# Order of TensorE's work at the end of the attention, in a cross-attention and two-layer local-attention block

## The chip, the cores and the metric

The kernel runs on one core of one Trainium2 chip. The metric is the device time of one execution in microseconds (us); the median of several runs is compared.

## The reference, cut to what matters

There are eight sequences of 256 rows by 256 columns, all float32. A gated cross-attention comes first. Then a small transformer of two layers runs over every sequence. One layer, cut to its core (H is 8 heads of 64, the window is 128 rows, and the hidden width of the feed-forward part is 682):

```python
h = shift_token(x)
q, k, v = split(h @ wqkv)
q, k = rotary_xpos(l2norm(q) * qs, l2norm(k) * ksc)
o = local_attention(q, k, v)
x = x + o @ wo                                   # "output product"
h = layernorm(shift_token(x)) * lg + lb
a, g = split(h @ w1 + b1)
x = x + (a * gelu(g)) @ w2 + b2                  # "down product"
```

## The kernel before, in words

Every engine has an instruction stream written out by hand, and semaphores hold the streams together; there is no scheduler. After the cross-attention come 17 **steps** (`run_steps`, each engine has its own `step(s, la, lf)`). Step s does two things at once: the attention of item s (`la` is its layer) and the feed-forward part of item s-1 (`lf` is its layer). Items 0 to 7 are the eight sequences in layer 0, items 8 to 15 are the same in layer 1. Step 0 has attention only (`lf` is None), steps 1 to 8 have `lf` 0, steps 9 to 15 have `lf` 1, and step 16 has the feed-forward part only. Steps 2 to 7 and 9 to 14 are hardware loops; the others are written out.

The weight products run as three float32r matmuls for each product (`split_product`, line 422): high by high, high by low, low by high. So each activation and each weight exists as a high part (`_hi`, copied by ScalarE) and a low part (`_lo`, subtracted by VectorE or GpSimd).

The end of a step on TensorE, in the order of the code: for each head h, `tr_probs(h)` (lines 609 to 611) transposes the probabilities; after every second head `weighted(pair)` (lines 623, 627) multiplies them by the values; pieces of the down product of item s-1 (`down(n)`, 12 pieces of three matmuls) stand between them. Behind the last head, 7, come `weighted(3)`, the four transposes of the next item's rows (`y_next`, line 415, PSUM bank 0), the last two down pieces (10 and 11, bank 7), and then the output product: two row tiles by four pairs of heads by three matmuls, 24 matmuls, row tile outermost, all in bank 2.

The three other engines at this place, each in this order:

- ScalarE: `heads_out(3)` (line 871) copies the result of `weighted(3)` as `oT_hi`; then `evac_yT` (line 800) copies the transposed next rows as `yT_hi`; in steps 0 and 8 `high_parts` (line 754) then copies the high parts of the next feed-forward weights.
- VectorE: `low_oT(3)` (line 1150) makes `oT_lo`; `low_yT` (line 1054) makes `yT_lo`; line 1259 adds the residual to the down product (called **yo** below); where `lf` is 1, line 1263 applies the gate and the second residual (**yo2**); line 1270 adds the residual to the output product and gives **x1**; in steps 0 and 8 `low_parts` (line 1039) then makes the low parts of the first feed-forward layer's weights.
- SyncE issues the loads and stores: the store of the finished rows waits for `res_done`, the load of `y_res` for `x1_done`, and the load of `y_next` for `y_tr`.

The next step begins on TensorE with `project(0, (0,))` (six matmuls of 512 columns, waits for `yT_done`), then `shift_rows` (lines 645 to 647, waits for x1), then the other projections. VectorE waits for `shift_rows` and starts its row statistics (line 1175); from these GpSimd and ScalarE make the normalised rows `hn` (line 883), which TensorE transposes.

Of the kernel before, what the change touches and what calls it, by code (L numbers as in the profile page):

```python
# [18 lines left out]
P = 128  # L19
# [3 lines left out]
ALU = mybir.AluOpType  # L23
# [6 lines left out]
HEADS, DH = 8, 64  # L30
# [4 lines left out]
def wait(eng, semaphore, value):  # L35

    if isinstance(value, int) and value <= 0:
        return
    eng.wait_ge(semaphore, value)
# [10 lines left out]
def build(nc, x, ctx_in, mask, g_xattn, g_ffn, Wq, bq, Wk, bk, Wv, bv, ln_gamma, ln_beta,  # L50
          wqkv, q_scale, k_scale, wo, ln_g, ln_b, w1, b1, w2, b2, rot_tab, win_mask, ident_in, shift_in, out):
    NB, S, D = x.shape
    T = S // P
# [3 lines left out]
    PAIRS = HEADS // 2  # L57
# [7 lines left out]
    STEPS = DEPTH * NB  # L65
# [10 lines left out]
    with st:  # L76
        def sb(name, shape, dt=F32):
            return st.enter_context(nc.sbuf_tensor(name, shape, dt))

        def sem(name):  # L80
            return st.enter_context(nc.semaphore(name))
# [5 lines left out]
        wo_hl = [sb(f"wo_{n}", [P, PAIRS, D], F32R) for n in ("hi", "lo")]  # L87
# [43 lines left out]
        y_next = sb("y_next", [P, T, D])  # L131
        y_res = sb("y_res", [P, T, D])
# [15 lines left out]
        oT = [sb(f"oT_{n}", [P, PAIRS, S], F32R) for n in ("hi", "lo")]  # L148
        x1 = sb("x1", [P, T, D])
# [13 lines left out]
        ps = st.enter_context(nc.psum_tensor("ps", [P, 8, 512], F32))  # L163

        def bank(i):
            return ps[:, i, :]

        def halves(i):
            return ps[:, i, :].rearrange("p (t n) -> p t n", t=2)
# [23 lines left out]
        ynext_in, yres_in, xm_in, res_stored = (  # L193
            sem(n) for n in ("ynext_in", "yres_in", "xm_in", "res_stored"))
# [213 lines left out]
        def _(pe):  # L408
            mm = nc.tensor.matmul

            def transpose_rows(src, b):

                for k in range(KC):
                    for t in range(T):
                        last = nc.tensor.transpose(bank(b)[:, k * S + t * P:k * S + t * P + P],  # L415
                                                   src[:, t, k * P:(k + 1) * P], ident[:])
                return last

            def split_product(out, lhsT, rhs, start, stop):

                for i, (a, b) in enumerate(((0, 0), (0, 1), (1, 0))):
                    last = mm(out, lhsT(a), rhs(b), start=(start and i == 0), stop=(stop and i == 2))  # L422
                return last
# [98 lines left out]
            def step(s, la, lf):  # L522
                f = s - 1

                def project(t, parts):

                    i = 0 if t == 0 else 3
                    if t == 0 and 0 in parts:
                        pe.wait_ge(yT_done, s + 1)
                        if isinstance(s, int) and s == 0:  # L530
                            pe.wait_ge(xnT_done, NB)
                            pe.wait_ge(kT_x, KC * NB)
                            pe.wait_ge(qT_x, KC * NB)
                            pe.wait_ge(v_x, NB)
                    elif 0 in parts:
                        wait(pe, pT_done, HEADS * s)
                    for j in parts:
                        if j == 2:
                            if t == 0:
                                wait(pe, x1_done, s)  # L540
                            else:
                                wait(pe, o_done, PAIRS * s)
                        if t == 0 and isinstance(s, int) and s in (0, NB):
                            pe.wait_ge(w_ready, VPIECES * la + j + 1)
                        o = bank(i + j) if j < 2 else bank(2 + 4 * t)
                        for k in range(KC):
                            c0 = k * YTC - k + t * P
                            last = split_product(o, lambda a: yT[a][:, c0:c0 + P],
                                                 lambda a: wqkv_hl[a][:, k, j * INNER:(j + 1) * INNER],
                                                 k == 0, k == KC - 1)  # L550
                        last.then_inc((qk_mm, qk_mm, v_mm2)[j], 1)
# [35 lines left out]
                def scores_own(pair):  # L587

                    for h in (2 * pair, 2 * pair + 1):
                        if h >= SB:  # L590
                            pe.wait_ge(mn_done, T * (HEADS * s + h - SB + 1))
                    for h in (2 * pair, 2 * pair + 1):
                        r = slice(h % 2 * DH, h % 2 * DH + DH)
                        mm(bank(h % SB)[:, 0:P], qT[r, pair, 0:P], kT[r, pair, 0:P], start=True, stop=True)  # L594

                def scores_both(pair):

                    for h in (2 * pair, 2 * pair + 1):
                        r = slice(h % 2 * DH, h % 2 * DH + DH)
                        mm(bank(h % SB)[:, P:3 * P], qT[r, pair, P:S], kT[r, pair, :], start=True, stop=True)\  # L600
                            .then_inc(s_mm2, 1)

                def tr_probs(h):

                    b, p = bank(3 + h % 2), pr[:, h % NS, :]
                    pe.wait_ge(pn_done, T * (HEADS * s + h + 1))
                    if h >= 2:
                        pe.wait_ge(pT_done, HEADS * s + h - 1)
                    nc.tensor.transpose(b[:, 0:P], p[:, 2 * P:3 * P], ident[:])  # L609
                    nc.tensor.transpose(b[:, P:2 * P], p[:, 0:P], ident[:])  # L610
                    nc.tensor.transpose(b[:, 2 * P:3 * P], p[:, P:2 * P], ident[:]).then_inc(pt_tr, 1)  # L611
# [41 lines left out]
                if A:  # L653
                    project(0, (0,))
                if F:
                    shift_rows()
                if A:
                    project(0, (1,))
# [31 lines left out]
                def downs(upto):  # L690

                    nonlocal n
                    while F and n < upto:
                        down(n)
                        n += 1

                if A:
                    pe.wait_ge(q_done, s + 1)
                    pe.wait_ge(k_done, T * s + 1)
                    pe.wait_ge(v_done, T * (s + 1))  # L700
                    scores_own(0)
                    pe.wait_ge(q1_done, s + 1)
                    pe.wait_ge(k_done, T * (s + 1))
                    scores_both(0)
                    downs(5)
                    for h in range(HEADS + 1):
                        if h in (0, 1, 3):
                            scores_own((h + 3) // 2)
                            scores_both((h + 3) // 2)
                        if h == 0:  # L710
                            downs(7)
                        if h < HEADS:
                            tr_probs(h)
                        if isinstance(s, int) and s in (0, NB) and h == HEADS - 1:
                            bias_products(la)
                        downs(min(10, 7 + (h + 1) // 2))
                        if h and h % 2 == 0:
                            weighted(h // 2 - 1)
                    if not (isinstance(s, int) and s == STEPS - 1):
                        pe.wait_ge(ynext_in, 16 * (s + 2))  # L720
                        pe.wait_ge(mn_done, T * HEADS * (s + 1))
                        transpose_rows(y_next, 0).then_inc(y_tr, 1)
                if F:
                    while n < T * HC:
                        down(n)
                        n += 1
                if A:
                    pe.wait_ge(o_done, PAIRS * (s + 1))
                    if isinstance(s, int) and s in (0, NB):
                        pe.wait_ge(w_ready, VPIECES * la + FIRST)  # L730
                        pe.wait_ge(b1_done, 3 * (la + 1))
                    for t in range(T):
                        for c in range(PAIRS):
                            last = split_product(bank(2)[:, t * D:(t + 1) * D],
                                                 lambda a: oT[a][:, c, t * P:(t + 1) * P],
                                                 lambda a: wo_hl[a][:, c, :], c == 0, c == PAIRS - 1)
                    last.then_inc(wo_mm, 1)

            run_steps(pe, step)


# [202 lines left out]
        def _(dve):  # L944
            V = nc.vector
# [130 lines left out]
            def step(s, la, lf):  # L1076
# [188 lines left out]
                if A:  # L1265
                    dve.wait_ge(wo_mm, s + 1)
                    dve.wait_ge(yres_in, 16 * (s + 1))
                    wait(dve, hn_done, s)
                    wait(dve, xb_done, s)
                    V.tensor_tensor(x1[:], halves(2), y_res[:], ALU.add).then_inc(x1_done, 1)  # L1270
                if isinstance(s, int) and s in (0, NB):
                    dve.wait_ge(b1_done, 3 * (la + 1))
                    low_parts(la, False, slice(LAST_W2 - FIRST, None))
# [192 lines left out]
```

## Time and profile before

| | us |
|---|---|
| median of 3 runs | 802.25 |
| lowest and highest run | 800.89, 802.79 |
| the profiled execution, its own time | 802.92 |
| its span, first to last instruction | 801.1 |

The mean granted TensorE clock of the profiled execution is 0.964 of full speed. The page gives busy times of each engine over the span; a timeline gives single instructions in order of time: start, duration, engine, line, operation, what is written and read, how many are merged in the row, and in brackets the idle time of the engine before it with what ended it. PE is TensorE's matmuls, PEld its weight loads, DVE is VectorE, ACT is ScalarE, POOL is GpSimd. Starts of neighbouring rows give the pace of an engine better than durations do, since instructions of one engine overlap at their ends.

### The profile page before, as it was taken

What the parts mean: (1) busy time and instruction counts of PE and PEld (TensorE: products, weight loads), DVE (VectorE), ACT (ScalarE), POOL (GpSimd) and SP (SyncE); (2) the same over time, 40 slices, a digit from 0 to 9 for tenths busy, and PEclk for the clock granted to TensorE, in tenths of its full rate; (3) what the DMA queues carried; (4) which work ended last, traced back from release to release, by engine and by line L of the source; (5) the groups of instructions that cost most, each with busy time, mean ns of one, the idle gap of its engine ahead of it and who ended that gap; (6) DMA issues with size and microseconds to landing.
All of it is one profiled execution on the core that took longest, in us unless ns stands there. A gap on an engine that the chain in (4) does not pass through costs nothing.

```text
span 801.1 us, 17081 instructions
## 1 busy us (share of the span) xinstructions
PE 726.8 (91%) x4984; PEld 604.8 (75%) x4984; DVE 532.6 (66%) x1486; ACT 481.9 (60%) x1289; POOL 439.9 (55%) x592
## 2 busy tenths in 40 slices
PE   6998875999999999999999899999999999999967
PEld 5787753777878787878787779778787878787846
DVE  2888897285858585757585854858585857575732
ACT  2333523468585858585757683757575757575842
POOL 0433553375556565656574564838383847474722
PEclk9999985799999999999999997999999999999999
DMA  6444330460101010101010101010101010101000
GB/s 213 145 144 157 111 65 27 133 226 13 41 2 39 0 39 0 39 0 39 0 39 1 39 2 53 1 54 0 52 0 52 0 52 0 52 0 40 1 27 13
DMA packets 32786, 38.36 MB, mean 48 GB/s; under 512 B 8476, under 2 KB 22896, under 8 KB 32752
## 3 DMA queue, kind: packets, MB, share of 16 engines
q1 hardware_dynamic: 32752, 37.95, 14.9%
q8 instruction: 16, 0.26, 0.1%
q14 instruction: 18, 0.15, 0.1%
HBM read 29.55 MB, written 8.39 MB: 47 GB/s over the span
## 4 chain that ended last, share of the span: by engine, by line
PE 55%; ACT 9%; issue 7%; DVE 7%; POOL 3%; DMA 1%; DVEq 0%; SPq 0%; ACTq 0%; POOLq 0%
PE ps L422 35%; PE ps L623 4%; ACT pr L860 4%; PE ps L582 3%; PE ps L609 2%; PE ps L600 2%; PE ps L517 2%; PE ps L594 2%; POOL pr L1372 2%; ACT pT L866 1%; PE ps L415 1%; DVE hT_lo L1130 1%; PE ps L627 1%; ACT hT_hi L899 1%; DVE sm L1157 1%
## 5 line engine op out<-in xcount | busy, mean ns | idle before, releaser
L1372 POOL TENSOR_SCALAR pr<-pr,rl 128x128 f32<-128x128 f32 (+1 forms) x256 | 106.9, 432 | 56.8 <-DVE rl L1163 56.5
L860 ACT ACTIVATE pr<-sm,mn 128x128 f32<-128x128 f32 (+1 forms) x256 | 113.8, 448 | 15.6 <-DVE mn L1157 14.5
L422 PE MATMUL ps<-hT_hi,w_hi 128*128 128x256 f32 (+1 forms) x352 | 105.0, 298 | 3.5 <-DVE hT_lo L1130 1.4
L1157 DVE CUSTOM_DVE_ANT_0 sm<-ps,wmask 128x128 f32<-128x128 f32 (+1 forms) x256 | 80.1, 355 | 34.5 <-PE ps L600 30.5
L422 PE MATMUL ps<-hT_hi,w_lo 128*128 128x256 f32 (+1 forms) x352 | 99.8, 284 | 0.0
L422 PE MATMUL ps<-hT_lo,w_hi 128*128 128x256 f32 (+1 forms) x352 | 99.0, 281 | 0.0
L1340 POOL TENSOR_TENSOR rn<-ss,nhalf 128x16 f32<-128x16 f32 x32 | 95.2, 2974 | 2.7
L820 ACT ACTIVATE sqb<-ps 128x512 f32<-128x512 f32 x64 | 38.0, 596 | 94.3 <-PE ps L422 88.6
L1354 POOL TENSOR_TENSOR u_lo<-u_pair,u_hi 128x256 fp32r<-128x256 f32 x64 | 74.1, 1166 | 25.3 <-ACT u_hi L841 15.6
L422 PE MATMUL ps<-wqkv_hi,yT_hi 128*128 128x512 f32 x192 | 80.0, 417 | 7.8 <-DVE arena L1002 5.3
L1285 POOL TENSOR_SCALAR hrs<-hmv 128x2 f32<-128x2 f32 x16 | 3.1, 193 | 151.5 <-DVE hmv L1180 151.5
L422 PE MATMUL ps<-wqkv_hi,yT_lo 128*128 128x512 f32 x192 | 77.2, 402 | 0.0
L422 PE MATMUL ps<-wqkv_lo,yT_hi 128*128 128x512 f32 x192 | 77.1, 402 | 0.0
L422 PEld LDWEIGHTS ps<-hT_hi,w_hi 128*128 128x128 f32 (+1 forms) x352 | 66.3, 188 | 11.0 <-DVE hT_lo L1130 10.4
L832 ACT ACTIVATE gl<-ps,b_sb 128x256 f32<-128x256 f32 x80 | 38.1, 476 | 53.6 <-PE ps L422 53.6
L422 PEld LDWEIGHTS ps<-hT_lo,w_hi 128*128 128x128 f32 (+1 forms) x352 | 66.8, 190 | 0.0
L422 PEld LDWEIGHTS ps<-hT_hi,w_lo 128*128 128x128 f32 (+1 forms) x352 | 66.2, 188 | 0.0
L422 PE MATMUL ps<-w_hi,u_hi 128*128 128x256 f32 x192 | 62.8, 327 | 0.7 <-POOL u_lo L1354 0.7
L866 ACT ACTIVATE pT<-ps 128x384 f32<-128x384 f32 x128 | 61.5, 483 | 2.4 <-PE ps L611 0.9
L1150 DVE TENSOR_TENSOR oT_lo<-ps,oT_hi 128x256 fp32r<-128x256 f32 x64 | 27.1, 424 | 48.8 <-ACT oT_hi L871 47.2
L422 PE MATMUL ps<-w_hi,u_lo 128*128 128x256 f32 x192 | 54.2, 282 | 0.0
L623 PE MATMUL ps<-pT,vs 128*64 128x256 f32 x256 | 42.7, 412 | 12.4 <-ACT pT L866 9.0
(150 smaller groups left out, 2098.0 us busy)
## 6 DMA issues: line engine op xcount, KB each, us to landing
arena<-x SPq DMA_DIRECT2D x16, 256.0 KB, 3.4
ystream<-arena SPq DMA_DIRECT2D x16, 256.0 KB, 2.1
y_next<-ystream SPq DMA_DIRECT2D x16, 256.0 KB, 2.7
y_res<-ystream SPq DMA_DIRECT2D x16, 256.0 KB, 2.6
arena<-L_ffn_w SPq DMA_DIRECT2D x6, 640.0 KB
arena<-ctx SPq DMA_DIRECT2D x8, 256.0 KB, 3.8
arena<-mask_BxSxS_ik SPq DMA_DIRECT2D x8, 256.0 KB, 2.8
xmid<-arena SPq DMA_DIRECT2D x8, 256.0 KB, 2.0
```

The costliest lines, as they stand in the source:

```text
L422: last = mm(out, lhsT(a), rhs(b), start=(start and i == 0), stop=(stop and i == 2))
L582: last = nc.tensor.transpose(bank(i + j)[:, c * P:(c + 1) * P], t1[:, t, j * INNER + c * P:j * INNER + (c + 1) * P], ident[:])
L623: mm(b[j * DH:(j + 1) * DH, 0:S], vs[:, 0, h * DH:(h + 1) * DH], pT[:, h % 4, P:3 * P], start=True, stop=False)
L820: A(sqb[:, j * INNER:(j + 1) * INNER], bank(i + j), ACT.Square).then_inc(sq_done, 1)
L832: A(gl[:, c % 2, :], ps[:, 5 + c % 2, S:2 * S], ACT.Gelu, bias=b1_sb[:, lf, 1, c:c + 1]).then_inc(gl_done, 1)
L860: A(pr[:, h % NS, a:b], sm[:, h % NS, a:b], ACT.Exp, bias=mn[:, h, t:t + 1], scale=-1.0, accum_out=ls[:, h, t:t + 1]).then_inc(e_done, 1)
L866: A(pT[:, h % 4, :], bank(3 + h % 2)[:, 0:3 * P], ACT.Copy).then_inc(pT_done, 1)
L1150: V.tensor_tensor(oT[1][:, pair, :], bank(5 + pair % 2)[:, 0:S], oT[0][:, pair, :].bitcast(F32), ALU.subtract).then_inc(o_done, 1)
L1157: V.tensor_tensor_reduce(sm[:, h % NS, a:b], bank(h % SB)[:, a:b], wmask[:, a:b], 1.0, -NEG, ALU.add, ALU.min, mn[:, h, t:t + 1]).then_inc ...
L1340: G.tensor_tensor(rn[:, t, :], ss[:, t, :], nhalf[:], ALU.pow).then_inc(rn_done, 1)
L1354: G.tensor_tensor(u[1][0:r, c, :], u_full[c % 4][0:r, :], u[0][0:r, c, :].bitcast(F32), ALU.subtract).then_inc(u_done, 1)
L1372: G.tensor_scalar(pr[:, h % NS, a:b], pr[:, h % NS, a:b], rl[:, h, t:t + 1], 1.0, ALU.mult, ALU.mult).then_inc(pn_done, 1)
```

## The change

`weighted(3)` leaves the loop over the heads. Behind the last transposes of probabilities now stand: the last two down pieces, the transposes of the next rows, the output product of pairs 0 and 1, `weighted(3)`, and the output product of pairs 2 and 3. The output product takes the pair as its outer loop and the row tile as its inner one, with row tile 0 in bank 1 and row tile 1 in bank 2; before each pair it waits for that pair's `o_done` alone. x1 (line 1270 before) reads the two banks. `project` gets a wait for `x1_done` ahead of the second projection of the first row tile, which uses bank 1. Nothing is added or removed: the same matmuls run in another order. The other engines' streams stay as they are, but for the operand of x1.

```diff
                     for j in parts:
+                        if j == 1 and t == 0:
+                            wait(pe, x1_done, s)
                         if j == 2:
...
-                        if h and h % 2 == 0:
+                        if h and h % 2 == 0 and h < HEADS:
                             weighted(h // 2 - 1)
+                if F:
+                    while n < T * HC:
+                        down(n)
+                        n += 1
+                if A:
                     if not (isinstance(s, int) and s == STEPS - 1):
                         pe.wait_ge(ynext_in, 16 * (s + 2))
                         pe.wait_ge(mn_done, T * HEADS * (s + 1))
                         transpose_rows(y_next, 0).then_inc(y_tr, 1)
-                if F:
-                    while n < T * HC:
-                        down(n)
-                        n += 1
-                if A:
-                    pe.wait_ge(o_done, PAIRS * (s + 1))
+
+                    def out_products(pairs):
+
+                        for c in pairs:
+                            pe.wait_ge(o_done, PAIRS * s + c + 1)
+                            for t in range(T):
+                                last = split_product(bank(1 + t)[:, 0:D],
+                                                     lambda a: oT[a][:, c, t * P:(t + 1) * P],
+                                                     lambda a: wo_hl[a][:, c, :], c == 0, c == PAIRS - 1)
+                        return last
+
+                    pe.wait_ge(mn_done, T * HEADS * (s + 1))
                     if isinstance(s, int) and s in (0, NB):
                         pe.wait_ge(w_ready, VPIECES * la + FIRST)
                         pe.wait_ge(b1_done, 3 * (la + 1))
-                    for t in range(T):
-                        for c in range(PAIRS):
-                            last = split_product(bank(2)[:, t * D:(t + 1) * D],
-                                                 lambda a: oT[a][:, c, t * P:(t + 1) * P],
-                                                 lambda a: wo_hl[a][:, c, :], c == 0, c == PAIRS - 1)
-                    last.then_inc(wo_mm, 1)
+                    out_products(range(0, 2))
+                    weighted(PAIRS - 1)
+                    out_products(range(2, PAIRS)).then_inc(wo_mm, 1)
...
-                    V.tensor_tensor(x1[:], halves(2), y_res[:], ALU.add).then_inc(x1_done, 1)
+                    V.tensor_tensor(x1[:], ps[:, 1:1 + T, 0:D], y_res[:], ALU.add).then_inc(x1_done, 1)
```

TensorE's stream before, at the end of a layer-1 loop step (steps 9 to 14), from the transposes of head 7 on; `w2` rows are down pieces, `wo` rows the output product:

```order
L609 MATMUL ps<-ident,pr 128x128
L610 MATMUL ps<-ident,pr 128x128
L611 MATMUL ps<-ident,pr 128x128
L618 REGISTER_ALU
L623 MATMUL ps<-pT,vs 64x256 x2
L627 MATMUL ps<-pT,vs 64x128 x2
L720 ISA
L721 REGISTER_ALU
L415 MATMUL ps<-ident,y_next 128x128 x4
L422 MATMUL ps<-w2_hi,u_hi 128x256
```

Behind the last row stand the rest of the two down pieces and the 24 output matmuls. The same stream with the change, first the transposes of the next rows and what follows them, in which the output product of pair 0 begins:

```order
L422 MATMUL ps<-w2_hi,u_lo 128x256
L727 ISA
L728 REGISTER_ALU
L415 MATMUL ps<-ident,y_next 128x128 x4
L422 MATMUL ps<-wo_hi,oT_hi 128x256
L422 MATMUL ps<-wo_lo,oT_hi 128x256
L422 MATMUL ps<-wo_hi,oT_lo 128x256
```

The down pieces and the transposes now stand ahead of `weighted(3)`. Then the place where `weighted(3)` stands now, between pair 1 and pair 2 of the output product:

```order
L422 MATMUL ps<-wo_hi,oT_lo 128x256
L625 MATMUL ps<-pT,vs 64x256 x2
L629 MATMUL ps<-pT,vs 64x128 x2
L734 REGISTER_ALU
L422 MATMUL ps<-wo_hi,oT_hi 128x256
```

Twelve output matmuls stand ahead of `weighted(3)`, twelve behind it. VectorE's stream at the same place, as it stands before (with the change the order is the same and only the line numbers are higher by 10), for a step with `lf` 1:

```order
L1150 TENSOR_TENSOR oT_lo<-ps,oT_hi 128x256
L1052 REGISTER_ALU
L1054 TENSOR_TENSOR yT_lo<-ps,yT_hi 128x2x256
L39 REGISTER_ALU
L1259 TENSOR_TENSOR arena<-ps,arena 128x512
L1261 REGISTER_ALU
L1262 REGISTER_ALU
L1263 SCALAR_TENSOR_TENSOR arena<-arena,tg 128x512
L1267 REGISTER_ALU
L1270 TENSOR_TENSOR x1<-ps,y_res 128x512
```

Nothing moved here: yT_lo, yo, yo2 and x1 stand behind oT_lo of pair 3, as before.

## Rows read from the trace of the kernel before

**Rows 1.** The page, busy time of each engine, and the chain that ended last by engine.

```profile
PE 726.8 (91%) x4984; PEld 604.8 (75%) x4984; DVE 532.6 (66%) x1486; ACT 481.9 (60%) x1289; POOL 439.9 (55%) x592
...
PE 55%; ACT 9%; issue 7%; DVE 7%; POOL 3%; DMA 1%; DVEq 0%; SPq 0%; ACTq 0%; POOLq 0%
```

**Rows 2.** Timeline of PE, end of step 12 and start of step 13.

```profile
645.87 0.27 PE L611 MATMUL ps<-ident,pr 128*128 128x128 f32 x1
645.90 0.36 PE L422 MATMUL ps<-w_hi,u_hi 128*128 128x256 f32 x1
...
648.23 0.27 PE L611 MATMUL ps<-ident,pr 128*128 128x128 f32 x1
649.16 0.65 PE L623 MATMUL ps<-pT,vs 128*64 128x256 f32 x4 [0.66 <-ACT pT L866]
...
649.96 0.66 PE L415 MATMUL ps<-ident,y_next 128*128 128x128 f32 x4
650.37 0.36 PE L422 MATMUL ps<-w_hi,u_hi 128*128 128x256 f32 x1
...
651.15 0.28 PE L422 MATMUL ps<-wo_hi,oT_hi 128*128 128x256 f32 x1
...
654.00 0.39 PE L422 MATMUL ps<-wqkv_hi,yT_hi 128*128 128x512 f32 x1
...
655.39 0.38 PE L645 MATMUL ps<-x,shift 128*128 128x128 f32 x2
```

**Rows 3.** Timeline of ACT, the same step.

```profile
646.27 0.37 ACT L871 ACTIVATE oT_hi<-ps 128x256 fp32r<-128x256 f32 x1
646.54 0.94 ACT L866 ACTIVATE pT<-ps 128x384 f32<-128x384 f32 x2
...
650.09 0.38 ACT L871 ACTIVATE oT_hi<-ps 128x256 fp32r<-128x256 f32 x1 [1.07 <-PE ps L627]
650.65 0.60 ACT L800 ACTIVATE yT_hi<-ps 128x512 fp32r<-128x512 f32 x1 [0.17 <-PE ps L415]
```

**Rows 4.** Timeline of DVE: x1 of step 11, then the same step 12 (`lf` 1).

```profile
614.82 0.69 DVE L1270 TENSOR_TENSOR x<-ps,y_res 128x512 f32<-128x512 f32 x1 [0.94 <-PE ps L422]
...
650.51 0.42 DVE L1150 TENSOR_TENSOR oT_lo<-ps,oT_hi 128x256 fp32r<-128x256 f32 x1 [1.58 <-ACT oT_hi L871]
651.28 0.69 DVE L1054 TENSOR_TENSOR yT_lo<-ps,yT_hi 128x512 fp32r<-128x512 f32 x1 [0.35 <-ACT yT_hi L800]
651.89 0.68 DVE L1259 TENSOR_TENSOR arena<-ps,arena 128x512 f32<-128x512 f32 x1
652.70 0.75 DVE L1263 SCALAR_TENSOR_TENSOR arena<-arena,tg 128x512 f32<-128x512 f32 x1
654.39 0.69 DVE L1270 TENSOR_TENSOR x<-ps,y_res 128x512 f32<-128x512 f32 x1 [0.94 <-PE ps L422]
```

**Rows 5.** Timeline of DVE, x1 at the end of step 2 (`lf` 0).

```profile
243.53 0.69 DVE L1270 TENSOR_TENSOR x<-ps,y_res 128x512 f32<-128x512 f32 x1 [1.82 <-PE ps L422]
```

**Rows 6.** Timeline of PE, end of step 15 (no transposes of next rows).

```profile
767.83 0.65 PE L623 MATMUL ps<-pT,vs 128*64 128x256 f32 x4 [0.58 <-ACT pT L866]
...
769.67 0.39 PE L422 MATMUL ps<-wo_hi,oT_hi 128*128 128x256 f32 x1
...
773.56 0.49 PE L645 MATMUL ps<-x,shift 128*128 128x128 f32 x2 [0.78 <-DVE x L1270]
```

**Rows 7.** End of step 8 and start of step 9: PE, ACT, DVE, PE.

```profile
486.19 1.12 PE L623 MATMUL ps<-pT,vs 128*64 128x256 f32 x4
...
490.17 4.10 ACT L754 ACTIVATE w_hi<-arena 128x1280 fp32r<-128x1280 f32 x4 [0.74 <-PE ps L422]
...
494.23 3.78 DVE L1039 TENSOR_TENSOR w_lo<-arena,w_hi 128x1386 fp32r<-128x1386 f32 x2
...
502.93 0.66 PE L415 MATMUL ps<-ident,hn 128*128 128x128 f32 x4 [1.70 <-ACT hn L883]
```

**Rows 8.** Busy times by stretch, step 8: us and busy us per engine, then PEclk, DMA share, GB/s.

```profile
486.00:489.00 3.00, 3.00 (x16) 2.27 (x16) 0.81 (x4) 0.56 (x2) 2.53 (x2) 0.50 0.00 0
```

More of the change, by code:

```diff
@@ L716, in step @@
                         downs(min(10, 7 + (h + 1) // 2))
-                        if h and h % 2 == 0:
+                        if h and h % 2 == 0 and h < HEADS:
                             weighted(h // 2 - 1)
[L719 to L722, printed above, removed]
                 if F:
@@ L727, in step @@
                 if A:
-                    pe.wait_ge(o_done, PAIRS * (s + 1))
+                    if not (isinstance(s, int) and s == STEPS - 1):
+                        pe.wait_ge(ynext_in, 16 * (s + 2))
+                        pe.wait_ge(mn_done, T * HEADS * (s + 1))
+                        transpose_rows(y_next, 0).then_inc(y_tr, 1)
+                    def out_products(pairs):
[6 more added lines that the diff above has]
+                        return last
+                    pe.wait_ge(mn_done, T * HEADS * (s + 1))
                     if isinstance(s, int) and s in (0, NB):
```

## The prediction, as made before the change was measured

> **What bounds the kernel now.** I read the page first [rows 1]: TensorE is busy for 91% of the span and holds 55% of the chain that ended last, twice as much as ScalarE, VectorE, GpSimd and the issue time together. So the time is the length of TensorE's stream, and a change is worth what it takes out of TensorE's idle time less what it puts in. From the x1 of step 11 to that of step 12, 614.82 to 654.39, are 39.57 us [rows 4], and the other loop steps repeat it, so one step can stand for many, and small sums count by the number of steps.
>
> Then I read the end of one loop step on each engine. On TensorE [rows 2] the last transpose of probabilities starts at 648.23, and `weighted(3)` only at 649.16, with 0.66 us idle in front of it: it waits for ScalarE's copy pT. That is the hole that the change can fill. Behind it TensorE has no gap: next rows, two down pieces, 24 output matmuls, the next step's first projection at 654.00, and `shift_rows` at 655.39. On VectorE [rows 4] oT_lo, yT_lo, yo and yo2 follow `weighted(3)` one after another, and x1 comes after 0.94 us of idle time. With `lf` 0 there is no yo2 and the idle time is 1.82 us [rows 5]. These two numbers are VectorE's slack against TensorE, and the change spends it, since all of that work stands behind `weighted(3)`, which comes later now.
>
> **The sum for one loop step.** W is the start of `weighted(3)`; before, it is 649.16.
>
> 1. TensorE up to W. Down pieces may start 0.03 us behind the start of the last transpose, as 645.87 to 645.90 shows. Two of them take 650.37 to 651.15, 0.78. The four transposes take 649.96 to 650.37, 0.41. Twelve output matmuls take half of 651.15 to 654.00, 1.42, and 0.08 more since the first product behind transposes is slower (0.78 against 0.71 for six) [rows 2]. A switch to the small products of `weighted` I price at 0.09 by the same kind of penalty, between 0 and 0.2. So W is 648.23 + 0.03 + 0.78 + 0.41 + 1.50 + 0.09 = 651.04, 1.88 later than before. pT is ready long before: the idle time of 0.66 us is gone.
> 2. TensorE behind W. Only pair 2's six matmuls are ready there. Pair 3 needs ScalarE and VectorE first. The end of step 15 shows exactly this pattern, `weighted(3)`, six matmuls, then a wait for oT_lo: from 767.83 to 769.67, 1.84 us [rows 6]. Six more take 0.78, so the next step's first projection could start at W + 2.62 = 653.66 against 654.00. Of the 0.66 us hole and the pause around it, about a third of a microsecond is left as gain; the rest comes back as a new wait for pair 3 and two more switches between kinds of products.
> 3. The same moment by yT. `heads_out(3)` starts 0.93 behind W (650.09 less 649.16). Its wait for the transposes of the next rows is gone, so yT_hi starts 0.27 later, the distance between 646.27 and 646.54, takes 0.60, and yT_lo starts 0.03 after it, as now (650.65 + 0.60 to 651.28), so at W + 1.83 [rows 3, 4]. It ends at W + 2.52, just in time for W + 2.62. There is 0.1 us to spare.
> 4. x1 with `lf` 0. yo comes 0.61 after yT_lo, at W + 2.44, and x1 another 0.61 later, at W + 3.05; it ends at W + 3.74. `shift_rows` follows six projections, 1.39 us (654.00 to 655.39), so at W + 4.01 = 655.05. x1 is ready. **Gain 0.34 us per step**; I take 0.32, between 0.1 and 0.4.
> 5. x1 with `lf` 1. yo2 comes 0.81 behind yo, at W + 3.25. x1 needs the engine, 0.67 later (0.75 less the overlap of 0.08 that 651.28, 0.69 long, and 651.89 show): W + 3.92. It ends at W + 4.61, and `shift_rows` starts 0.05 later, at 655.70 (as in step 15, where it follows a late x1) [rows 4, 6], with a first product slower by some 0.1, an estimate by the penalty of item 1. In effect `shift_rows` is finished as if it had begun at 655.81, against 655.39. **Loss 0.42 us per step.** TensorE stands idle for about 0.6 us in front of `shift_rows` instead of in front of `weighted(3)`. Everything of the next step hangs on `shift_rows` or on TensorE's order behind it, so the loss isn't made up. Bounds: 0.1 if everything on VectorE runs closer than the rows show, 0.7 if nothing overlaps.
>
> A rule of the Trainium skill bears on item 5: "VectorE: DVE Perf Modes", section "The DRAIN you can't avoid", says that the next operation on VectorE does not start until the pipe of the one before is empty. By that rule alone the step would lose about 0.2 us more. The trace does not follow it to the letter here, with starts 0.61 us apart for operations of 0.69 us (yT_lo and yo) [rows 4].
>
> **The steps that are not in that pattern.** In step 15 there are no next rows, and x1 waits for nothing but yo2 and the products; by the same items it gains 0.3. Behind steps 0 and 8 the high parts of the weights stand on ScalarE behind yT_hi, and VectorE's low parts need the third of them before the row statistics can begin. TensorE waits for what follows, 1.70 us in step 9 [rows 7], so a delay there counts in full. In step 8 the clock is at 0.50 of full, which is the 1.2 GHz level [rows 8], because the bias products of single columns came before; the run ahead of W, 2.69 us at full clock, takes about 4.9 there (estimate, 1.8 times). W is then 486.19 + 4.9 = 491.1, the high parts start 0.93 + 0.27 + 0.5 later, at 492.8 instead of 490.17, and the third ends about 2.75 us on, at 495.5. The low parts began at 494.23 [rows 7]. **Loss 1.3 in step 8.** In step 0 no down pieces stand ahead: I take 0.8. Both lie between 0 and 2; a clock that rises sooner, since dense products come sooner, makes them smaller.
>
> The added wait for x1 in `project` costs nothing: `shift_rows`, ahead of it, waits for the same. The two banks cost nothing either: one instruction reads both, and it waits for the last product anyway. SyncE's store of the finished rows moves back with yo2 by over 1 us, and the load of `y_res` behind it has most of a step before it is needed; `y_next` is asked for behind x1 too.
>
> **Sum.** Seven steps with `lf` 0 (1 to 7): -2.2. Step 15: -0.3. Six steps with `lf` 1 (9 to 14): +2.5. Step 0: +0.8. Step 8: +1.3. Together +2.1 us. On the profiled execution's 802.92 that is 805.0, on the median of the runs, 0.7 below it, 804.4. About 0.2%, 1.6 us, is what a measurement of this kernel can tell from no change.
>
> **Rivals.**
>
> - A, faster: VectorE and ScalarE keep up in all steps, and each of 15 steps keeps 0.32 us. Against it speak the 0.94 us of slack with `lf` 1, of which W moving back by 1.88 asks twice as much; for it, that TensorE is the engine of the chain. 802.25 - 4.8 = 797.5. The Trainium skill's "Perfetto Trace Analysis", section "Optimization Strategies", argues this way: the goal is a matmul engine as highly utilized as possible. It would have the filled hole count as a gain. Chance 0.15.
> - B, no change: steps 1 to 15 as summed, but behind steps 0 and 8 the clock rises sooner or the delayed weights find cover. -2.2 - 0.3 + 2.5 = 0, so 802.3. Chance 0.15.
> - C, clearly slower: also with `lf` 0 x1 or yT_lo comes too late. There yT_lo has 0.1 us to spare and x1 0.2, so if VectorE's chain is longer by over 0.2 us from W, the gain of seven steps goes and `lf` 1 loses 0.6. 6 x 0.6 and the 2.1 of steps 0 and 8 are +5.7: 808. Chance 0.12. The Trainium skill's rule quoted in item 5 leads here, if it held in full.
> - D, the hole isn't filled, because another wait holds TensorE ahead of W. Of the output product's operands oT_lo of pair 1 would be the one; it is done over 1 us before its use. Under 0.03.
>
> My forecast, slower through late x1 and late weights while `lf` 0 steps gain, has 0.55. Its own range is 802.5 to 806.5, a third of it within 0.2%.
>
> **Chances and range.** Faster: A and a little of the forecast's edge, 0.17. Same: B and a third of the forecast, 0.30. Slower: the rest with C, 0.53. The predicted time is the forecast's 804.4. The range from 800.2 to 807.0 takes in B and most of C and leaves out A.
>
> **What the changed profile should show.** No idle time in front of `weighted(3)`, which starts 1.9 us later behind the last transpose; about 0.2 us idle in front of pair 3's first product; with `lf` 1 about 0.6 us idle in front of `shift_rows`, released by x1, and no idle time in front of x1 but full occupation from yT_lo on; with `lf` 0 no wait at `shift_rows`. Loop steps of 39.25 us with `lf` 0 and 40.0 with `lf` 1, against 39.57. A longer wait for hn in steps 1 and 9. I am wrong if the layer-1 steps are shorter than before, or if step 9 doesn't start its statistics later.

## The result, and the profile after the change

| | before | changed |
|---|---|---|
| median, us | 802.52 (6 runs) | 809.44 (6 runs) |
| lowest and highest run | 800.89, 805.09 | 806.8, 812.93 |
| the profiled execution, its own time | 802.92 | 812.93 |
| its span | 801.1 | 811.0 |
| its mean granted clock | 0.964 | 0.955 |

Changed over before is 1.0099, with a 95% interval of 1.0078 to 1.0119: slower by 6.9 us. The prediction said 804.4, and its range ended at 807.0. The profiled execution of the changed kernel is the slowest of its six, 3.5 us over their median. So its parts below add up to more than 6.9.

The page of the changed kernel, busy times and chain by engine:

```profile
PE 736.0 (91%) x4984; PEld 611.3 (75%) x4984; DVE 533.8 (66%) x1486; ACT 479.4 (59%) x1289; POOL 436.7 (54%) x592
...
PE 53%; ACT 10%; DVE 8%; issue 8%; POOL 3%; DMA 1%; DVEq 1%; ACTq 0%; SPq 0%; POOLq 0%
```

Against [rows 1] the same 4984 matmuls are busy for 9.2 us longer. Part of that is the order itself. These are the windows from one x1 to the next of a layer-1 loop step, first of the kernel before, then of the changed one (columns as in [rows 8]; the clock is at 1.00 in both):

```profile
614.82:654.39 39.57, 38.03 (x282) 31.61 (x281) 27.23 (x78) 26.90 (x74) 23.91 (x32) 1.00 0.09 27
622.66:662.71 40.05, 38.61 (x282) 31.72 (x280) 27.14 (x79) 26.75 (x74) 23.85 (x32) 1.00 0.08 26
```

TensorE is busy 0.58 us longer per step with `lf` 1, and with `lf` 0 it is 38.36 against 38.01. Over steps 1 to 7 and 9 to 14 that makes about 6 of the 9.2 us (estimate). So busy time tells little here; the mean clock, 0.955 against 0.964, is the better hint.

**A loop step.** TensorE at the end of step 12, timeline, answering to [rows 2]:

```profile
655.98 0.27 PE L613 MATMUL ps<-ident,pr 128*128 128x128 f32 x1
656.01 0.37 PE L422 MATMUL ps<-w_hi,u_hi 128*128 128x256 f32 x1
...
658.77 0.65 PE L625 MATMUL ps<-pT,vs 128*64 128x256 f32 x4
...
659.57 0.38 PE L422 MATMUL ps<-wo_hi,oT_hi 128*128 128x256 f32 x1
...
660.26 0.28 PE L422 MATMUL ps<-wo_hi,oT_lo 128*128 128x256 f32 x1
660.61 0.38 PE L422 MATMUL ps<-wo_hi,oT_hi 128*128 128x256 f32 x1
...
661.42 0.45 PE L422 MATMUL ps<-wqkv_hi,yT_hi 128*128 128x512 f32 x1
...
663.52 0.48 PE L647 MATMUL ps<-x,shift 128*128 128x128 f32 x2 [0.49 <-DVE x L1280]
```

The hole in front of `weighted(3)` is gone, and a new one of 0.49 us stands at `shift_rows`, released by x1. VectorE in the same step, answering to [rows 4]:

```profile
660.13 0.42 DVE L1160 TENSOR_TENSOR oT_lo<-ps,oT_hi 128x256 fp32r<-128x256 f32 x1 [3.44 <-ACT oT_hi L881]
660.62 0.69 DVE L1064 TENSOR_TENSOR yT_lo<-ps,yT_hi 128x512 fp32r<-128x512 f32 x1
661.23 0.68 DVE L1269 TENSOR_TENSOR arena<-ps,arena 128x512 f32<-128x512 f32 x1
662.04 0.75 DVE L1273 SCALAR_TENSOR_TENSOR arena<-arena,tg 128x512 f32<-128x512 f32 x1
662.71 0.68 DVE L1280 TENSOR_TENSOR x<-ps,y_res 128x512 f32<-128x512 f32 x1
```

From yT_lo to x1 the profile shows no wait. Between one x1 and the next lie 39.27 us with `lf` 0 and 40.04 with `lf` 1, against 39.57 before. Six steps of +0.47, seven of -0.30 and the -0.56 of step 15 come to +0.2, close to the forecast 0. So the 6.9 us are not here.

**Steps 0 and 8.** The distances from x1 to x1 show the place. Step 1 takes 44.38 us (before 41.58), and step 9 takes 46.87 (before 42.06). Timeline of VectorE at the end of step 8, with the row statistics of step 9 behind it, answering to [rows 7]:

```profile
495.70 0.68 DVE L1280 TENSOR_TENSOR x<-ps,y_res 128x512 f32<-128x512 f32 x1
497.27 4.91 DVE L1049 TENSOR_TENSOR w_lo<-arena,w_hi 128x1386 fp32r<-128x1386 f32 x2 [0.89 <-ACT w_hi L764]
502.11 0.28 DVE L1185 BATCH_NORM_STATS2 hst<-x 128x6 f32<-128x128 f32 x1
```

ScalarE, GpSimd and TensorE at the same place:

```profile
494.34 4.08 ACT L764 ACTIVATE w_hi<-arena 128x1280 fp32r<-128x1280 f32 x4
495.70 5.02 POOL L1377 TENSOR_TENSOR w_lo<-arena,w_hi 128x1280 fp32r<-128x1280 f32 x2 [4.81 <-ACT w_hi L764]
...
507.10 1.12 PE L415 MATMUL ps<-ident,hn 128*128 128x128 f32 x4 [3.95 <-ACT hn L893]
```

The low parts of the weights are late, as forecast. But they also take 4.91 us where they took 3.78, and TensorE's wait for hn is 3.95 us where it was 1.70 [rows 7]. The windows of the changed kernel (columns as in [rows 8]):

```profile
495.00:500.00 5.00, 5.00 (x28) 4.25 (x28) 4.11 (x4) 4.50 (x6) 4.30 (x2) 1.00 0.54 193
500.00:505.00 5.00, 3.15 (x14) 2.22 (x12) 4.96 (x11) 0.60 (x1) 1.82 (x4) 1.00 0.06 18
505.00:510.00 5.00, 2.90 (x9) 2.52 (x10) 4.35 (x7) 4.27 (x8) 4.65 (x4) 0.62 0.00 0
510.00:515.00 5.00, 5.00 (x31) 4.81 (x31) 3.63 (x6) 1.70 (x5) 3.99 (x2) 0.70 0.01 3
```

And of the kernel before, over the same stage:

```profile
500.00:505.00 5.00, 3.29 (x16) 2.10 (x14) 4.67 (x8) 4.15 (x9) 4.59 (x6) 1.00 0.00 0
505.00:510.00 5.00, 4.89 (x40) 4.78 (x41) 4.94 (x9) 3.08 (x7) 4.75 (x3) 1.00 0.01 3
510.00:515.00 5.00, 5.00 (x44) 4.85 (x42) 4.22 (x7) 3.50 (x9) 4.76 (x5) 1.00 0.00 2
```

The granted clock is at the 1.2 GHz level for part of the last two stretches. Before, with the short wait, it stayed at full. The counts of matmuls, 40 against 84, are not of the same work, since this stage begins 4.2 us later in the changed kernel. The clock falls while TensorE still waits, about 1 us before the transposes of hn:

```profile
506.00:507.00 1.00, 0.00 (x0) 0.00 (x0) 0.96 (x3) 1.00 (x4) 1.00 (x1) 0.60 0.00 0
```

### The profile page after: what moved, and what is told of

It is laid out like the page before. It is cut to its first block, busy times and chain, and to the rows that moved or that the text cites. A ratio compares the mean times of both kernels' runs of the same rounds, so it can differ in the third digit from the quotient of the medians.

```text
span 811.0 us, 17122 instructions
## 1 busy us (share of the span) xinstructions
PE 736.0 (91%) x4984; PEld 611.3 (75%) x4984; DVE 533.8 (66%) x1486; ACT 479.4 (59%) x1289; POOL 436.7 (54%) x592
## 2 busy tenths in 40 slices
DMA packets 32786, 38.36 MB, mean 47 GB/s; under 512 B 8476, under 2 KB 22896, under 8 KB 32752
## 4 chain that ended last, share of the span: by engine, by line
PE 53%; ACT 10%; DVE 8%; issue 8%; POOL 3%; DMA 1%; DVEq 1%; ACTq 0%; SPq 0%; POOLq 0%
PE ps L422 33%; ACT pr L870 4%; PE ps L625 3%; PE ps L584 3%; PE ps L611 2%; PE ps L602 2%; PE ps L517 2%; PE ps L596 2%; POOL pr L1382 2%; PE ps L629 1%; PE ps L415 1%; DVE hT_lo L1140 1%; DVE sm L1167 1%; ACT hT_hi L909 1%; DVE oT_lo L1160 1%
## 5 line engine op out<-in xcount | busy, mean ns | idle before, releaser
L422 PEld LDWEIGHTS ps<-hT_hi,w_hi 128*128 128x128 f32 (+1 forms) x352 | 68.0, 193 | 9.5 <-DVE hT_lo L1140 9.3
L881 ACT ACTIVATE oT_hi<-ps 128x256 fp32r<-128x256 f32 x64 | 24.0, 376 | 74.7 <-PE ps L629 74.7
```

## The experiments

Two theories stood at the start. **W:** the loss comes from steps 0 and 8, through the late weights. **L:** it comes from the loop steps, through the late x1 of layer 1.

### 1. The new order everywhere but in steps 0 and 8

```diff
-                    out_products(range(0, 2))
-                    weighted(PAIRS - 1)
-                    out_products(range(2, PAIRS)).then_inc(wo_mm, 1)
+                    if (isinstance(s, int) and s in (0, NB)):
+                        pe.wait_ge(o_done, PAIRS * (s + 1))
+                        out_products(range(PAIRS)).then_inc(wo_mm, 1)
+                    else:
...
```

The last down pieces and `weighted(3)` have their old places in these two steps too.

> The change in all steps but 0 and 8, which keep the order of before (products still in two banks). Theory W (nearly all of the loss comes from the late weight parts behind steps 0 and 8 and what follows in steps 1 and 9): 802.5 us, between 801 and 804, with steps 1 and 9 as long as before (41.6 and 42.1 us from x1 to x1), since steps 1 to 7 and 15 gain 2.5 us and steps 9 to 14 lose 2.5 to 2.9. Rival L (the late x1 in the layer-1 loop costs most): over 806 us.

Measured: 802.08 against 802.23, ratio 1.0002 (0.9987 to 1.0017). The loop steps are as in the changed kernel (39.27 and 40.04), and steps 1 and 9 take 41.01 and 42.65 us. **Theory W holds, and L falls.** Thirteen new loop steps and step 15 cost nothing in sum that the measurement could tell.

### 2. The new order in steps 0 and 8 alone

The condition of the first experiment turned round.

> The new order only in steps 0 and 8, the order of before in all others. Theory W: 808 to 810 us, steps 1 and 9 together 6 to 8 us longer than before, with a wait for the normalised rows of over 3.5 us in both. Rival L: at most 803 us.

Measured: 808.35, ratio 1.0089 (1.0066 to 1.0112), 6.1 us more than before. Steps 1 and 9 take 45.63 and 45.05 us, together 7.0 more than before, and TensorE waits 3.70 and 3.95 us for hn in them. Two steps of seventeen make nearly the whole loss.

### 3. High parts of the weights first

```diff
+                    if isinstance(s, int) and s in (0, NB):
+                        high_parts(la, False)
                     heads_out(PAIRS - 1)
                     ...
-                if isinstance(s, int) and s in (0, NB):
-                    high_parts(la, False)
```

The change, but ScalarE makes the high parts ahead of the copies of `weighted(3)`, in the time in which it has nothing to do.

> The change, and in steps 0 and 8 ScalarE copies the high parts of the feed-forward weights before it copies the result of the last weighted values, while it would sit idle. Theory W: the loss of steps 1 and 9 goes, 801 to 803 us; VectorE's two low parts, which no longer overlap with GpSimd's, take under 3.5 us where they took 4.91, and the wait for the normalised rows is under 2 us. Rival L: 808 us, no gain of over 1.5.

Measured: 800.26, ratio 0.9983 (0.9962 to 1.0004); against the changed kernel's 809.44 that is 9.2 us. The interval takes in 1, so this kernel can't be called faster than the one before. Step 1 takes 40.98 us and step 9 takes 41.93. The low parts now take 3.10 us for the same two operations. The tile `w_lo` in step 0, in the changed kernel (durations in ns, minimum, median and maximum, then first and last start):

```profile
L1377 POOL TENSOR_TENSOR w_lo<-arena,w_hi x2: 2118/2538/2959, 163.2 to 166.1; 128x1280 fp32r<-128x1280 f32 x1, 42x256 fp32r<-42x256 f32 x1
L1049 DVE TENSOR_TENSOR w_lo<-arena,w_hi x2: 2142/2495/2848, 164.7 to 167.5; 128x1386 fp32r<-128x1386 f32 x2
```

And in this experiment, where GpSimd's part is over before VectorE's begins:

```profile
L1377 POOL TENSOR_TENSOR w_lo<-arena,w_hi x2: 726/1824/2921, 158.4 to 161.2; 128x1280 fp32r<-128x1280 f32 x1, 42x256 fp32r<-42x256 f32 x1
L1049 DVE TENSOR_TENSOR w_lo<-arena,w_hi x2: 1592/1594/1597, 163.0 to 164.5; 128x1386 fp32r<-128x1386 f32 x2
```

Alone, VectorE needs 1.60 us for one and GpSimd 2.92 and 0.73. Together they seem to take turns. GpSimd's first runs from 163.16 to 166.12. VectorE's first, started at 164.73, ends at 164.73 + 2.85 = 167.58, 1.46 behind that. GpSimd's small one starts at 166.1 and ends at 168.2, 0.65 behind VectorE's first. VectorE's second ends at 169.64, 1.4 behind that. Each end is the end of the other engine's operation plus nearly the full length of one's own. This can be tested by itself (experiment 9).

### 4. x1 ahead of yo2

```diff
-                    if lf == 1:
-                        ... yo2 ...
                     V.tensor_tensor(x1[:], ps[:, 1:1 + T, 0:D], y_res[:], ALU.add).then_inc(x1_done, 1)
+                if lf == 1:
+                    ... yo2 ...
```

> The change, and VectorE makes x1 before the second residual of the finished rows (yo2) where lf is 1. By the rows, each of steps 9 to 14 loses its late x1 (0.45 us) and keeps the gain of the layer-0 steps (0.3 us): 6 x 0.75 = 4.5 us less than the change, 804 to 806 us; loop steps of 39.27 us in layer 1. Rival: if something else than x1 holds shift_rows in layer 1, no more than 1 us less than the change.

Measured: 809.01, ratio 1.0086 (1.006 to 1.0112). The expectation failed. Layer-1 steps fell only from 40.04 to 39.74, and TensorE's timeline in step 12 says why:

```profile
660.24 0.49 PE L647 MATMUL ps<-x,shift 128*128 128x128 f32 x2 [0.19 <-DVE arena L1279]
```

The releaser is now yo2, not x1: `shift_rows` also waits for `res_done`, which in layer 1 only yo2 sets. I had moved one of two operations that TensorE waits for. The 6 x 0.30 us that the trace shows as gain are not to be seen in the time, 809.01 against 809.44; the intervals of the two ratios are wider than the difference.

### 5. Both mends, with the wait put right

```diff
                     pe.wait_ge(x1_done, s)
-                    wait(pe, res_done, f)
+                    if lf == 1:
+                        pe.wait_ge(yo_done, s - NB)
+                    else:
+                        wait(pe, res_done, f)
```

Experiments 3 and 4 together. `res_done` guards bank 7 here, which yo has read already, so `yo_done` is enough (its count gets one added in step 8, where yo still counts for `res_done`).

> Both mends: ScalarE's high parts first in steps 0 and 8, x1 ahead of yo2, and shift_rows waits in layer 1 for yo instead of yo2 (bank 7 is free from yo on; in the kernel with x1 first it was yo2 that released shift_rows, 0.19 us late, and the loop steps took 39.74 us). Theory: layer-1 loop steps take 39.27 us as those of layer 0, 0.77 less than with the change; 6 x 0.77 = 4.6 us below the kernel with the high parts first (800.3): 795 to 797 us. Rival: a third wait takes the place (yT_lo), and the steps stay over 39.6: 798 to 800 us.

Measured: **796.24**, ratio 0.9925 (0.991 to 0.994), faster than both kernels. Steps 1 and 9 take 40.99 and 41.16 us, and the layer-1 steps 39.39. Against the third experiment layer 1 gives 6 x 0.64 = 3.8 us by the trace, and 4.0 by the times (800.26 less 796.24). The time came out as expected, though the steps did not quite reach the expected 39.27. The new order of VectorE's end of a step:

```profile
646.60 0.68 DVE L1272 TENSOR_TENSOR arena<-ps,arena 128x512 f32<-128x512 f32 x1
647.19 0.68 DVE L1278 TENSOR_TENSOR x<-ps,y_res 128x512 f32<-128x512 f32 x1
647.79 0.74 DVE L1282 SCALAR_TENSOR_TENSOR arena<-arena,tg 128x512 f32<-128x512 f32 x1
```

`shift_rows` then starts at 648.24 without a wait for yo2.

### 6. The kernel before, with late weights

```diff
                 if isinstance(s, int) and s in (0, NB):
+                    act.wait_ge(wo_mm, s + 1)
                     high_parts(la, False)
```

TensorE's order is the old one, and the high parts wait for the output product.

> The kernel before, in which ScalarE in steps 0 and 8 waits for the end of the output product before it copies the high parts, about 3.5 us later than it did. No instruction on TensorE moves. If late weight parts alone make the loss of steps 1 and 9, both get longer by 2.5 to 5 us and the whole is 807 to 811 us; if it takes the new order on TensorE too, it stays under 804 us.

Measured: 811.97, ratio 1.0124 (1.0105 to 1.0142), 9.6 us slower, a little over what was expected. Late weights make the loss without any new order. The low parts take 4.90 us here too, and steps 1 and 9 take 46.43 and 47.19.

### 7 and 8. What the clock adds

The seventh is the changed kernel with step 9 written out in front of the loop, nothing else. It is the control for the eighth, which has this in steps 1 and 9, ahead of the transposes of hn:

```diff
+                if isinstance(s, int) and s in (1, NB + 1):
+                    for i in range(12):
+                        mm(bank(5), yT[0][:, 0:P], wqkv_hl[0][:, 0, 0:INNER], start=True, stop=True)
```

These twelve products are added work that nobody reads; they fill most of the wait.

> Control for the next: the change with step 9 written out instead of being the loop's first turn. 807 to 811 us, as the change; steps 1 and 9 long as there, clock at half after the wait for the normalised rows.

> The same with 12 products of 512 columns into the unused bank 5 in steps 1 and 9, ahead of the transposes of the normalised rows, where TensorE sits idle for 3.7 to 3.95 us; they take 2.8 us and their result is used nowhere. If part of the loss is the clock that falls in that wait, it stays at full speed, and steps 1 and 9 get shorter by 1 to 2.5 us together or each: 2 to 4 us less than the control. If the clock plays no part: the same time.

Measured: 807.99, ratio 1.0073 (1.0051 to 1.0095), and with the fill 807.0, ratio 1.0057 (1.0033 to 1.0082). The times don't tell the two apart. The traces do, for step 9. TensorE with the fill, then the windows with it:

```profile
500.92 2.97 PE L671 MATMUL ps<-wqkv_hi,yT_hi 128*128 128x512 f32 x12
504.80 0.66 PE L416 MATMUL ps<-ident,hn 128*128 128x128 f32 x4 [0.91 <-ACT hn L897]
```

```profile
500.00:505.00 5.00, 4.09 (x19) 3.02 (x18) 4.92 (x13) 2.42 (x6) 3.03 (x6) 1.00 0.02 3
505.00:510.00 5.00, 4.87 (x35) 4.25 (x34) 4.57 (x6) 3.65 (x7) 4.83 (x4) 1.00 0.00 0
```

The windows of the control:

```profile
500.00:505.00 5.00, 1.26 (x7) 0.89 (x5) 4.92 (x11) 3.10 (x7) 3.72 (x6) 0.77 0.00 0
505.00:510.00 5.00, 5.00 (x22) 4.42 (x21) 3.97 (x5) 2.72 (x5) 4.57 (x4) 0.55 0.01 3
```

The transposes come 11.19 us behind x1 in both, but with the fill the clock stays at the 2.4 GHz level, and step 9 takes 44.62 us instead of 45.95. In step 1 it is 43.90 against 44.38. So in these two executions the fallen clock costs 1.3 and 0.5 us. The expected 2 to 4 us in the time were too much.

What is left behind the wait when the clock stays up can be read too. From the start of the transposes of hn to the x1 of step 9 are 33.43 us with the fill, 34.77 in the control, 35.48 in the changed kernel and 32.76 before. Of the 0.67 us between the fill and before, 0.47 is the late x1 of layer 1. So 0.2 us remain.

The twelve profiled executions agree on when the clock falls. In the changed kernel and in experiments 2, 4, 6, 7 and 9, where TensorE waited 3.68 us or more for hn in both steps, the clock fell to the 1.2 GHz level in steps 1 and 9. Before, in experiments 1, 3, 5 and 10 (waits of 0.74 to 1.74 us) and with the fill it fell in neither.

### 9. GpSimd's low parts behind VectorE's

```diff
                 def low_w2(l):
+                    pool.wait_ge(w_ready, VPIECES * (l + 1))
```

> The change, with GpSimd's low parts in steps 0 and 8 (the two w_lo subtractions of GpSimd) put behind VectorE's two, so that the two engines never run such subtractions at the same time; the start of VectorE's low parts is left late. Theory of mutual exclusion (the two engines' operations that read two SBUF operands each run one after the other, never together): VectorE's two low parts take 3.1 us instead of 4.91, so from x1 to the row statistics are about 5.0 us instead of 6.6 (the first statistics), the wait for hn shrinks by 1.8 us in steps 1 and 9, and the median goes from about 809.4 to 804.5 to 806.5, if nothing waits for GpSimd's later low parts. Rival 1, their length comes from something else (ScalarE's copies at the same time, or the operands just written): they stay at 4.9 and the time at 809 to 811. Rival 2: GpSimd is now late for its part of hn (hmr): low parts 3.1, but hn no earlier, 808 to 811.

Measured: 809.78, ratio 1.0106 (1.0085 to 1.0126). VectorE and GpSimd in step 8, in order of time:

```profile
493.96 3.12 DVE L1049 TENSOR_TENSOR w_lo<-arena,w_hi 128x1386 fp32r<-128x1386 f32 x2 [0.89 <-ACT w_hi L764]
497.16 3.63 POOL L1378 TENSOR_TENSOR w_lo<-arena,w_hi 128x1280 fp32r<-128x1280 f32 x2 [8.72 <-DVE w_lo L1049]
500.88 0.19 POOL L1295 TENSOR_SCALAR hrs<-hmv 128x2 f32<-128x2 f32 x1
```

**The two engines' subtractions exclude each other:** VectorE's takes 3.12 us instead of 4.91, and GpSimd's 3.63 instead of 5.02, though VectorE's starts as late as in the changed kernel and ScalarE copies at the same time. The rival about ScalarE falls. But the second rival came true as well. GpSimd's own share of hn (`hrs`, and what follows it) now waits until 500.88, with the statistics there since 498.2, and the transposes of hn start 12.43 us behind x1 instead of 11.40. The order only moved the wait to the other engine.

### 10. The mends on the kernel before

Experiment 5's two mends, with TensorE's old order.

> The kernel before with the same two mends as the fifth experiment (high parts of the weights ahead of the copies of weighted(3) in steps 0 and 8; yo2 behind x1, with shift_rows waiting for yo instead of yo2 in layer 1), so the old order of TensorE's work. If the mends are worth something only because the new order makes VectorE late, layer-1 loop steps stay at 39.57, low parts shrink from 3.7 to 3.1 us in steps 0 and 8, and the time is 800.5 to 802 (before: about 802.3). Then the new order with both mends (796.24) owes about 5 us to the order itself: 0.30 us per layer-0 step and about 0.2 per layer-1 step in the trace, and the rest at steps 8 and 9. If the mends alone bring the time to 797 or less, the order is worth nothing.

Measured: 811.27, ratio 1.0103 (1.0084 to 1.0122). This was badly missed, by 10 us. TensorE and ScalarE in step 8:

```profile
497.73 0.58 PE L422 MATMUL ps<-wo_hi,oT_hi 128*128 128x256 f32 x1 [4.95 <-DVE oT_lo L1153]
...
492.88 4.07 ACT L757 ACTIVATE w_hi<-arena 128x1280 fp32r<-128x1280 f32 x4 [9.55 <-PE ps L422]
496.86 0.36 ACT L874 ACTIVATE oT_hi<-ps 128x256 fp32r<-128x256 f32 x1
```

In the old order `weighted(3)` is done early, and all of the output product waits for its copy. The high parts in front of that copy hold TensorE for 4.95 us in step 8 and 2.69 in step 0; step 8 takes 58.18 us instead of 52.26. The two waits together are 7.6 us of the 8.8 that the median lost. In the new order the same 4 us of ScalarE's work lie beside twelve output matmuls, and in step 8 beside down pieces too. x1 ahead of yo2 gains nothing either, 39.65 us per layer-1 step against 39.57. So these mends, as a pair, are worth something only with the new order, and the new order only with them. Not tested is whether high parts that come earlier still would help the old order; so how much of the 796.24 the order itself gives is open.

### The steps side by side

Worked out from the timelines of the profiled executions; "hn" is the start of the transposes of hn, "low" the start and length of VectorE's low parts.

| | x1 to low, steps 0 and 8 | low | x1 to hn | length of steps 1 and 9 | time |
|---|---|---|---|---|---|
| before | 0.61, 0.61 | 3.66, 3.78 | 8.97, 9.31 | 41.58, 42.06 | 802.5 |
| changed | 1.77, 1.57 | 4.91, 4.91 | 11.36, 11.40 | 44.38, 46.87 | 809.4 |
| 3 high first | 0.61, 0.60 | 3.10, 3.10 | 8.40, 8.63 | 40.98, 41.93 | 800.3 |
| 6 before, late | 2.93, 2.93 | 4.91, 4.90 | 12.53, 12.76 | 46.43, 47.19 | 812.0 |
| 8 fill | 1.78, 1.57 | 4.90, 4.91 | 11.36, 11.19 | 43.90, 44.62 | 807.0 |
| 9 GpSimd behind | 1.78, 1.57 | 3.12, 3.12 | 12.39, 12.43 | 45.13, 46.94 | 809.8 |

## Why the prediction was right in direction and too small

The step that failed is the term of the sum for steps 0 and 8: +0.8 and +1.3 us were forecast, 2.1 together, and experiment 2 measured 6.1. The working gave the delay of the low parts alone a price. It put at nothing that they would take longer beside GpSimd's, and that the longer wait would bring the clock down.

- **Items 1 and 2, TensorE up to and behind W.** Right. In step 12, W is 2.79 us behind the last transpose (forecast 2.81), and the first projection is 2.65 behind W (2.62). The forecast 0.2 us of idle time in front of pair 3's first product shows only as a gap between starts, 0.35 where 0.12 is the pace.
- **Item 3, yT_lo.** It starts at W + 1.85 (forecast 1.83). Right.
- **Item 4, `lf` 0.** Gain 0.30 us per step (0.32). Right.
- **Item 5, `lf` 1.** x1 at W + 3.94 (3.92), `shift_rows` after 0.49 us idle (0.6), loss 0.47 us per step (0.42). Right. Its remark that everything hangs on `shift_rows` was confirmed by experiment 5, which took the wait away and got the steps down to 39.39. That yo2 is itself a second wait for `shift_rows` was not in the working; it cost nothing in the forecast, but made experiment 4 miss.
- **Step 15.** Gain 0.56 (0.3), small.
- **The sum over the loop, 0.** Experiment 1 measured -0.15 us, with an interval of about 1.2 us to either side. Right.
- **The steps 0 and 8: here it failed.** The working was "+0.8" and "+1.3", "both lie between 0 and 2". In the profiled executions they cost about 3.6 and 4.8. Step 8, counted from the x1 of step 7, has W 4.81 us later (forecast 4.9), and the low parts start 1.40 later (1.3). So the delay was right there. In step 0 it was not: the low parts start 1.62 us later, twice the 0.8 taken without a working. No down pieces stand ahead, but the twelve output matmuls do, at the 1.2 GHz level, and W is 3.60 us later (both counted from the end of the bias products). Two terms that stand nowhere in the sum follow the delay. First, VectorE's low parts take 1.13 us longer (1.25 in step 0), since moved they lie wholly beside GpSimd's, and the two exclude each other (experiment 9). Second, "a delay there counts in full" was too little: TensorE's longer wait goes with a clock at its lower level. The transposes of hn start 2.53 later, the x1 of step 9 is 5.25 later, and with 0.47 for the layer-1 step 2.25 us are left that lie behind the wait. In step 0 the same count is 1.62, 1.25, and 0.71 behind the wait. Against its control, experiment 8 shows 1.3 and 0.5 us as the clock's, and with the clock kept up only 0.2 us are left behind the wait in either step. So most of the 2.25 and 0.71 goes with the clock; how long it stays low differs between executions.
- **The sign of the clock.** The prediction named the clock, but only as a help (dense products come sooner), and so its bounds lay on the wrong side.

In the profiled execution the two steps cost 8.4 us, and the last stretch, behind the last x1, is 1.2 longer (29.47 against 28.28), again with a lower clock (the page's row PEclk ends in 88, before in 99). In the medians experiment 2 puts the two steps at 6.1. The forecast's 2.1 was short by 4 to 5 us, and that is the miss.

The rivals: A (faster) and B (no change) fell, B because its condition, that the late weights find cover, was the opposite of what happened. C gave nearly the right time by the wrong mechanism: x1 of `lf` 0 is not late. The rule of the Trainium skill on the drain, quoted in item 5, would have cost 0.2 us more per layer-1 step; 0.61 us from yT_lo to yo and a loss of 0.47 don't show it. The Trainium skill's rule that a filled TensorE is the goal, quoted with rival A, would have given a gain. Here the filled hole brought 0.3 us a step where nothing downstream was late.

A page that I had not drawn on names the missing term. "SBUF — State Buffer", section "Who interferes with whom", in the Trainium skill, says that a VectorE instruction with two SBUF inputs contends with a GpSimd instruction that reads SBUF, that such contention is an exclusive lock, and that the issue order decides who blocks. The trace agrees: 1.60 us alone, 2.85 us behind GpSimd's.

## What to carry to other kernels

When work is moved later on the pacing engine, follow every producer behind it to the steps that are written out differently, and price there not only the later start but what the moved operation now lies beside: two-operand SBUF operations of VectorE and GpSimd don't overlap. Here a wait of TensorE that grew from 1.7 to 4 us cost more than its length, since the clock fell in it and stayed low for a while behind it. And a move and its mend are one edit: the high parts first gain 9 us in the new order, and with the mend of x1 they lose about as much in the old one. So an ordering is judged only with the streams of the other engines fitted to it.

## What the runs showed of the hardware that was not expected

- VectorE and GpSimd `TENSOR_TENSOR` operations whose two inputs are in SBUF run one after the other. A GpSimd subtraction on 42 partitions by 256 columns takes 0.72 to 0.74 us alone and 2.12 us when VectorE's stands in front of it; VectorE's of 128 by 1386 takes 1.60 us alone, and 2.85 and 2.14 in turns with GpSimd's. VectorE's x1 of step 8, which reads one input from PSUM, starts together with a GpSimd subtraction at 495.70 and takes 0.68 us, as elsewhere.
- In a TensorE wait of 3.95 us that ended at 507.10 the granted clock fell, and it was 0.62 over the stretch from 505 to 510 and 0.70 from 510 to 515; after a wait of 1.70 us, or with twelve unused products of 512 columns in the wait, it stayed at 1.00.
- Clock phases differ from one execution to the next: the changed kernel's six runs span 806.8 to 812.93 us with mean clocks of 0.954 to 0.963, so that single profiled executions can't be compared to better than some 3 us here. Step 8 shows it: its code is the same in the changed kernel and in the control of experiment 7, yet it took 52.70 us at a mean clock of 0.87 in the one, and 49.29 at 0.97 in the other.
